# Channel statistics of a two-layer metaformer kernel, two pixels to an instruction

## The reference

```python
# layer 0
x = x + _L0_conv_ref(_ln_c(x), ...)      # patches of 3x3 pixels, best match of 512 vectors, a small MLP
t = _to_tokens(x); t = t + _L0_ffn_ref(_ln_t(t), W1, b1, W2, b2); x = _from_tokens(t, x)
# layer 1
x = x + _L1_conv_ref(_ln_c(x))           # x / (2 + 1e-4 * box5x5(sum over channels of x*x)) ** 0.75
t = _to_tokens(x); t = t + _L1_ffn_ref(_ln_t(t), W1, b1, W2, b2); x = _from_tokens(t, x)

def _ln_c(v, eps=1e-6):                  # over the 96 channels of one pixel; _ln_t the same with 1e-5
    m = jnp.mean(v, axis=1, keepdims=True); s = jnp.var(v, axis=1, keepdims=True)
    return (v - m) / jnp.sqrt(s + eps)
```

## Time and profile before

| | |
|---|---|
| median of 3 runs | 3355.06 us (3355.01 to 3362.01) |
| profiled execution | 3366.41 us, its span 3364.6 us |
| mean granted TensorE clock | 0.957 |
| busy: DVE, PE, ACT, POOL | 3022.2, 2824.8, 2608.5, 1192.6 us |
| DVE's statistics (L815) | 3456 instructions, 634.3 us |
| chain that ended last, by engine | DVE 36%, ACT 26%, PE 25%, DMA 7%, issue 5% |

### The profile page before, as it was taken

One profiled execution on the slowest core, in us unless ns is written; L12 is line 12 of the kernel. 1 busy time (PEld: TensorE's weight loads), 2 busy tenths in 40 slices (PEclk: granted clock), 3 DMA queues, 4 the chain that ended last, 5 costly groups with the idle time before them and its releaser, 6 DMA issues.

```text
span 3364.6 us, 55888 instructions
## 1 busy us (share of the span) xinstructions
PE 2824.8 (84%) x15886; PEld 1512.2 (45%) x15886; DVE 3022.2 (90%) x10843; ACT 2608.5 (78%) x7047; POOL 1192.6 (35%) x1159
## 2 busy tenths in 40 slices
PE   5888898988888888888888888888989899889654
PEld 2444444444445444444444444444444445444322
DVE  6888999999999999999999999999999999999532
ACT  0444788888888887878888788888888888888876
POOL 1223243333334333333433433334343434334221
PEclk9999999999999999999999999999999999999755
DMA  3111222222222222232232222223222223232111
GB/s 91 48 55 47 66 69 84 80 72 81 71 73 80 69 83 66 69 82 67 68 84 65 73 79 68 84 68 83 71 82 71 83 70 84 68 84 58 37 48 43
DMA packets 236607, 237.32 MB, mean 71 GB/s; under 512 B 183426, under 2 KB 186764, under 8 KB 236300
## 3 DMA queue, kind: packets, MB, share of 16 engines
q1 hardware_dynamic: 226060, 214.86, 23.2%
q0 software_dynamic: 10240, 18.89, 2.2%
HBM read 134.72 MB, written 57.02 MB: 57 GB/s over the span
## 4 chain that ended last, share of the span: by engine, by line
DVE 36%; ACT 26%; PE 25%; DMA 7%; issue 5%; SPq 0%; POOL 0%; POOLq 0%; DVEq 0%
ACT ffn_hid L552 11%; ACT ffn_x L585 10%; PE banks L415 10%; DVE st L815 7%; DMA ffn_xT<-ffn_x 7%; DVE ffn_hid L911 7%; DVE pix L824 6%; DVE ffn_hid L903 6%; PE banks L392 4%; PE banks L460 4%; PE banks L400 3%; DVE x L894 3%; PE banks L438 2%; ACT h L665 2%; ACT x L598 1%
## 5 line engine op out<-in xcount | busy, mean ns | idle before, releaser
L552 ACT ACTIVATE ffn_hid<-banks 128x512 f16<-128x512 f32 (+1 forms) x2304 | 1052.7, 492 | 387.3 <-PE banks L392 386.6
L415 PE MATMUL banks<-wcT,xc 128*128 128x512 f32 x2304 | 1217.8, 620 | 79.7 <-DVE pix L824 43.6
L392 PE MATMUL banks<-ffn_xT,w1q 128*128 128x512 fp8e5 (+1 forms) x2304 | 706.7, 340 | 260.1 <-ACT ffn_hid L552 170.4
L1080 POOL TENSOR_TENSOR x<-x,ffn_f 128x864 f32<-128x864 f32 x256 | 491.7, 1921 | 1038.5 <-DVE nb L777 920.3
L824 DVE TENSOR_REDUCE pix<-banks 128x1 f32<-128x512 f32 x1152 | 787.1, 684 | 69.0 <-PE banks L415 68.7
L392 PEld LDWEIGHTS banks<-ffn_xT,w1q 128*128 128x128 bf16 x2304 | 219.5, 98 | 783.7 <-ACT ffn_hid L552 541.5
L400 PE MATMUL banks<-w2q,ffn_hid 128*128 128x96 bf16 x6912 | 394.6, 211 | 160.7 <-DVE ffn_hid L911 159.9
L903 DVE TENSOR_SCALAR ffn_hid<-ffn_hid,b1q 128x1152 f16<-128x1152 f16 x768 | 419.3, 559 | 116.0 <-ACT ffn_hid L552 116.0
L400 PEld LDWEIGHTS banks<-w2q,ffn_hid 128*128 128x128 f16 x6912 | 353.1, 101 | 364.1 <-issue 335.0
L598 ACT ACTIVATE x<-x,cols 128x96 f32<-128x96 f32 x1152 | 511.7, 473 | 0.0
L585 ACT ACTIVATE ffn_x<-x,cols 128x96 fp8e5<-128x96 f32 x1152 | 501.4, 485 | 0.0
(11 more groups left out here) (137 smaller groups left out, 2849.9 us busy)
## 6 DMA issues: line engine op xcount, KB each, us to landing
xt<-x_tok_in SPq DMA_DIRECT2D x128, 432.0 KB
xc<-x_chan_in SPq DMA_DIRECT2D x128, 432.0 KB
out_tok<-x SPq DMA_DIRECT2D x128, 432.0 KB
ffn_xT<-ffn_x SPq DMA_TRANSPOSE x256, 2.6
win<-x_tok_in,xrow POOLq DMA_INDIRECT x128, 3.1
wrow<-vector_table,vidx POOLq DMA_INDIRECT x128, 2.7
shift<-shift_in SPq DMA_DIRECT2D x1, 960.0 KB
vector_table<-wtab SPq DMA_DIRECT2D x1, 384.0 KB, 2.9
```

The costliest lines, as they stand in the source:

```text
L392: last = pe.matmul(bank[:, 0:c1 - c0], w1q[:, ffn.layer, c * P:(c + 1) * P], pairs, start=True, stop=True)
L415: last = pe.matmul(ps_score[score_bank(j)], xc[p][:, j, :], wcT[:, :], start=True, stop=True)
L552: return nc.scalar.activation(dst, src, ACT.Copy)
L1080: tt(dst, x, ffn.f[:, :, :], ALU.add).then_inc(ready, 1)
```

## The change

The statistics take two pixels at a time. The source is read channel by channel and within a channel pixel by pixel, so that the even places are all of the first pixel and the odd places all of the second; the six values are then count, mean and sum of squared deviations of two pixels. They go straight into `pix`, by kind (plane 0 the counts, 1 the means, 2 the sums, 3 the roots), so `st3`, `mtmp`, `twice` and five operations of `moments` go. Nine pixels are five instructions; the fifth reads the last pixel twice and fills a tenth place that nobody uses. The groups of 3+6, 9 and 3+3+3 pixels become 2+3, 5 and 2+1+2 instructions. Means in place of doubled means change the factors to -1.0, and one operation of `mlp_input` (L876) goes. The wait on `kept` moves from `moments` to the front of the statistics of x2. The roots and their arguments are addressed as four rows of nine, where `pix` has rows of ten.

```diff
@@ -165,17 +165,16 @@
         xt = sb("xt", [P, XT, J, C])
         xc = [sb(f"xc_{i}", [P, J, P]) for i in range(2)]
 
-        st3 = sb("st3", [P, 3, J, 6])
-
-        pix = [sb(f"pix_{i}", [P, 3, 4, J]) for i in range(2)]
-        twice = [b[:, 0, 0:3, :] for b in pix]
-        ssq = [b[:, 1, 0:3, :] for b in pix]
-        roots = [b[:, 2, :, :] for b in pix]
-
-        mx = [b[:, 1, 1, :] for b in pix]
-        mtmp = sb("mtmp", [P, 2, 3, J])
+
+
+        pix = [sb(f"pix_{i}", [P, 4, 4, 2 * PAIRS]) for i in range(2)]
+        mean = [b[:, 1, 0:3, 0:J] for b in pix]
+        ssq = [b[:, 2, 0:3, 0:J] for b in pix]
+        roots = [b[:, 3, :, 0:J] for b in pix]
+
+        mx = [b[:, 2, 1, 0:J] for b in pix]
         args = sb("args", [P, 4, J])
-        rtmp = sb("rtmp", [P, 4 * J])
+        rtmp = sb("rtmp", [P, 4, J])
         nb1 = sb("nb1", [P, J])
         sim = [sb(f"sim_{i}", [P, J]) for i in range(2)]
         top = [sb(f"top_{i}", [P, 8]) for i in range(2)]
@@ -206,7 +205,7 @@
 
 
         img = sb("img", [P, 3, SLOTS, J])
-        twice_i, ssq_i, rstd_i = (img[:, i, :, :].rearrange("p s j -> p (s j)") for i in range(3))
+        mean_i, ssq_i, rstd_i = (img[:, i, :, :].rearrange("p s j -> p (s j)") for i in range(3))
         r2_i, sq_i = sb("r2_i", [P, SLOTS * J]), sb("sq_i", [P, SLOTS * J])
 
         cols_i = sb("cols_i", [P, 4, SLOTS, J])
@@ -696,7 +695,8 @@
             nc.vector.memset(pow_half[:], -0.5)
             nc.vector.memset(eps[:, 0, :], 1e-5)
             nc.vector.memset(eps[:, 1:3, :], 1e-6)
-            nc.vector.memset(st3[:], 0.0)
+            for b in pix:
+                nc.vector.memset(b[:], 0.0)
             for c in chosen:
                 nc.vector.memset(c[:], 0.0)
 
@@ -770,49 +770,36 @@
                 if k.back is not None:
                     wait_past(dve, ffn0.x8_ready, k.back)
                 rc.begin(k.moments)
-                flat = lambda b: b.rearrange("p a j -> p (a j)")
-                y = flat(roots[k.p])
-                yield from inverse_root(rc, flat(args[:, :, :]), y, rtmp[:, :])
+                yield from inverse_root(rc, args[:, :, :], roots[k.p], rtmp[:, :, :])
                 rc.wait()
-                nc.vector.scalar_tensor_tensor(out=nb1[:, :], in0=twice[k.p][:, 0, :], scalar=-0.5,
+                nc.vector.scalar_tensor_tensor(out=nb1[:, :], in0=mean[k.p][:, 0, :], scalar=-1.0,
                                                in1=roots[k.p][:, 0, :], op0=ALU.mult,
                                                op1=ALU.mult).then_inc(root_ready, 1)
                 yield
 
-            MOMENTS = 7
+            MOMENTS = 2
             mc = Chain(dve, mom_chain, MOMENTS)
 
             def moments(tile, p):
-
 
                 dve.wait_ge(stats_ready, tile + 1)
                 wait_past(dve, root_ready, tile)
-                wait_past(dve, kept, tile - 6)
                 mc.begin(tile)
-                of = lambda i: st3[:, :, :, i]
-                d, m2 = mtmp[:, 0, :, :], mtmp[:, 1, :, :]
-                mc.add(nc.vector.tensor_tensor(d, of(1), of(4), ALU.subtract),
-                       nc.vector.tensor_tensor(m2, of(2), of(5), ALU.add))
-                yield
-                mc.wait()
-                mc.add(nc.vector.tensor_tensor(d, d, d, ALU.mult))
-                yield
-                mc.add(nc.vector.tensor_tensor(twice[p], of(1), of(4), ALU.add))
-                yield
-                mc.wait()
-                mc.add(nc.vector.scalar_tensor_tensor(out=ssq[p], in0=d, scalar=C / 4.0, in1=m2, op0=ALU.mult,
-                                                      op1=ALU.add))
-                yield
-                mc.wait()
                 mc.add(nc.vector.scalar_tensor_tensor(out=args[:, 0:3, :], in0=ssq[p], scalar=1.0 / C,
                                                       in1=eps[:, :, :], op0=ALU.mult, op1=ALU.add),
                        nc.vector.tensor_copy(args[:, 3, :], ssq[p][:, 1, :]))
                 assert mc.done == mc.per
                 yield
 
-            def group_stats(which, src, j0, j1, between):
-                for j in range(j0, j1):
-                    last = nc.vector.bn_stats(st3[:, which, j, :], src[:, j, :])
+            def group_stats(which, src, k, i0, i1, between):
+
+                if which == 2 and i0 == 0:
+                    wait_past(dve, kept, k.stats - 6)
+                for i in range(i0, i1):
+                    two = src[:, 2 * i:2 * i + 2, :] if 2 * i + 1 < J else src[:, J - 1:J, :].broadcast_to([P, 2, C])
+                    last = nc.vector.bn_stats(
+                        pix[k.q][:, 0:3, which, 2 * i:2 * i + 2].rearrange("p f t -> p t f"),
+                        two.rearrange("p t c -> p c t"))
                     run(between, 1)
                 return last
 
@@ -848,13 +835,13 @@
                 yield
                 f1c.wait()
                 one = pick[p][:, :].rearrange("p (o j) -> p o j", o=1).broadcast_to([P, 3, J])
-                f1c.add(nc.vector.tensor_tensor(junk[:, :, :], pix[p][:, :, 1, :], one, ALU.mult))
+                f1c.add(nc.vector.tensor_tensor(junk[:, :, :], pix[p][:, 1:4, 1, 0:J], one, ALU.mult))
                 yield
                 f1c.wait()
                 nc.vector.tensor_reduce(chosen[p][:, 0:3], junk[:, :, :], AX.X, ALU.add).then_inc(pick_ready, 1)
                 yield
 
-            f3c = Chain(dve, f3_chain, 6)
+            f3c = Chain(dve, f3_chain, 5)
 
             def win_vector(f2, q, between):
 
@@ -873,13 +860,12 @@
                 f3c.begin(f3)
                 f3c.add(nc.vector.tensor_reduce(dots[:, :], prod_dot[:, :, :], AX.X, ALU.add),
                         nc.vector.tensor_scalar(mix[:, 0:1], chosen[q][:, 2:3], top_q, None, ALU.mult),
-                        nc.vector.tensor_scalar(mix[:, 2:3], chosen[q][:, 0:1], 0.5, None, ALU.mult),
                         nc.vector.tensor_scalar(mix[:, 1:2], top_q, -1.0, 1.0, ALU.mult, ALU.add))
                 meanwhile()
                 f3c.wait()
 
                 f3c.add(nc.vector.tensor_tensor(inp[:, C:C + J], dots[:, :], roots[q][:, 3, :], ALU.mult),
-                        nc.vector.tensor_scalar(wnorm[:, :], win[q][:, :], mix[:, 2:3], mix[:, 0:1],
+                        nc.vector.tensor_scalar(wnorm[:, :], win[q][:, :], chosen[q][:, 0:1], mix[:, 0:1],
                                                 ALU.subtract, ALU.mult))
                 f3c.wait()
                 run(between, 1)
@@ -945,7 +931,7 @@
                 yield
                 lc.wait()
                 lc.add(nc.vector.tensor_scalar(alpha, rg, 1.0, None, ALU.add),
-                       nc.vector.scalar_tensor_tensor(out=beta, in0=twice_i, scalar=-0.5, in1=rg,
+                       nc.vector.scalar_tensor_tensor(out=beta, in0=mean_i, scalar=-1.0, in1=rg,
                                                       op0=ALU.mult, op1=ALU.mult))
                 yield
                 lc.wait()
@@ -961,7 +947,7 @@
                 yield from inverse_root(lc, arg, rstd, t)
                 lc.wait()
                 assert lc.done == lc.per
-                nc.vector.scalar_tensor_tensor(out=bias, in0=twice_i, scalar=-0.5, in1=rstd, op0=ALU.mult,
+                nc.vector.scalar_tensor_tensor(out=bias, in0=mean_i, scalar=-1.0, in1=rstd, op0=ALU.mult,
                                                op1=ALU.mult).then_inc(lrn_ready, 1)
                 yield
 
@@ -996,10 +982,10 @@
                 scores(2, WIN_TURN, factors, 2)
                 if k.fs is not None:
                     dve.wait_ge(xt_loaded[k.p], landed(k.fs, k.p))
-                    last = group_stats(1, xt[:, k.fs & XT - 1], 0, 3, factors)
+                    last = group_stats(1, xt[:, k.fs & XT - 1], k, 0, 2, factors)
                 if k.tail is not None:
                     dve.wait_ge(x2_ready, k.tail + 1)
-                    last = group_stats(2, x2[:, k.tail & RING - 1], 0, J, factors)
+                    last = group_stats(2, x2[:, k.tail & RING - 1], k, 0, PAIRS, factors)
                 if k.f2 is not None:
                     win_vector(k.f2, k.q, factors)
                 relu(ffn1, k.rear, 0)
@@ -1009,21 +995,21 @@
                 scores(5, 6, factors, 2)
                 round_up(ffn1, k.rear)
                 if k.fs is not None:
-                    last = group_stats(1, xt[:, k.fs & XT - 1], 3, J, factors)
+                    last = group_stats(1, xt[:, k.fs & XT - 1], k, 2, PAIRS, factors)
                 run(factors)
                 if k.f3 is not None:
                     residual1(k.f3, k.q)
                 scores(6, 7)
                 if k.f3 is not None:
                     dve.wait_ge(x1_ready, k.f3 + 1)
-                    group_stats(0, x1[k.q], 0, 3, iter(()))
+                    group_stats(0, x1[k.q], k, 0, 2, iter(()))
                 scores(7, 8)
                 if k.f3 is not None:
-                    group_stats(0, x1[k.q], 3, 6, iter(()))
```

(5 more changed lines are left out.)

## The result

| | before | after |
|---|---|---|
| median of 10 runs | 3359.06 us (3355.01 to 3365.66) | 3369.64 us (3362.88 to 3379.74) |
| ratio to before | | 1.0031, 95% interval 1.0018 to 1.0043 |
| profiled execution, its span | 3366.41, 3364.6 us | 3371.26, 3369.5 us |

What follows compares the result with a forecast made beforehand. DVE was busiest (3022 of 3364.6 us), with regular steps also closing through PE and ACT within some 0.1 us. Terms +62, -2, -8, -11 and -4 gave +37 on 3355: 3392 us, range 3305 to 3440 at about 0.8.

Steps and rivals of the forecast that it cites:

- The price of the statistics: BN_STATS on DVE: 192 values read alternately run at full rate, 344 ns, saving 0.44 us a step.
- The rival by hop cost: Alternating read on DVE pays for every hop, 460 ns per statistics instruction: 3351 us, chance 0.25.
- The race: DVE's rounding L911 against POOL's product L1075: index and product come 0.19 us earlier, so 35 more steps are lost.
- The tipping point: Lead at which POOL's product goes ahead of DVE's rounding: between zero and 0.1 us for POOL.
- 35 x (24.85 - 23.08) = +62 us: Regular steps: 35 of 44 races won by little flip, each step growing from 23.08 to 24.85 us.
- -0.3 each: The 27 regular steps already lost get shorter through fewer statistics, together -8 us.
- the joins: Five DVE operations removed between relu units of ffn0: 0.55 us of work, hidden behind ACT but for 0.1 us.
- the -8 and -2 of the sum: Regular steps: -8 us for 27 already lost, -2 for 9 still won and some 14 with a late vector.
- 14 x -0.3 = -4: Ramp and tail steps: 0.3 us less each, together -4 us.
- Image steps: 28 steps, two of eight, where the product comes too late to race: -0.4 us each, so -11 us.
- The race is still won: DVE's rounding still goes first in the 44 steps: 3325 us at full rate, or 3300; chance 0.18.
- 27 x -2.1 = -57: If the index comes 0.1 us later, the 27 lost steps are won too: -57 us, giving 3300.

Runs made afterwards that it cites:

- after_split32: Changed kernel with the five statistics of xt split 3+2 in place of 2+3, one moving ahead of the vector index: 3334.0 us, 0.9912.
- before_early: Kernel before, with the ninth statistics instruction of x2 moved from ahead of the vector index to behind it: 3359.7 us, 0.9996.
- before_nojoins: Kernel before without the five joining operations, so the norms are not computed: 3339.0 us, 0.9936.
- before_early2: Kernel before, with the ninth statistics instruction of x2 moved behind the first two relu operations of ffn1: 3414.7 us, 1.0163.
- before_order: Kernel before, with a wait that holds POOL's product until the rounding of ffn1 of the same step is done: 3318.8 us, 0.9883.
- after_joins: Changed kernel with five operations of 27 values, results unused, put where the joins stood: 3382.9 us, 1.0048.
- after_order: Changed kernel, with a wait that holds POOL's product until the rounding of ffn1 of the same step is done: 3283.9 us, 0.976.
- after_half: Changed kernel with POOL's product taken over four of the nine pixels: 3296.7 us, 0.9808.

## Why the prediction was right in its mechanism and too large in its size

**The price of the statistics** was right. I had the choice between 344 ns (full rate) and 460 (a hop on every value, after L794), and took the lower: 353. The rival by hop cost is out. The rule of the 16-byte lines that I cited from the Trainium skill, "SBUF — State Buffer", Specifications, does not show in this read: it never hits a line twice in a row, yet costs 0.02 ns a value (353 against 349 ns for 192). The page "Vector Engine (DVE) Microarchitecture Reference" of the Trainium skill, section 5.2, fits with its one-source operation that alternates between two regions at the full rate; here the regions are 384 bytes apart. L794's 17 ns over L798 were no price of its stride that BN_STATS shares.

**The race** was right: index 0.18 us earlier (0.19 forecast), rounding at the same place, 40 more races lost (35 forecast), 68 in all for a forecast of 62. The tipping point, between a lead of 0 and one of 0.1 us for POOL, can be narrowed over all traces: the product starting 0.026 us ahead of the rounding still had to stand back (after_split32), 0.029 us ahead it went first (before_early, before_nojoins). One link was wrong without consequence: I wrote that the product follows the index by a gather. It follows the relu pair behind the index (before_early and before_early2). In the change both move together.

**The term that was mis-sized** is "35 x (24.85 - 23.08) = +62 us". I took the length of a lost step from lost steps of the kernel before, and all 28 of those were steps that were late already when they lost: the rounding starts 12.94 us or more into them, not 12.65. In the step of the earlier trace rows the rounding starts 0.57 us later than in that of the earlier trace rows, the index ends only 0.30 later, because part of the delay goes into the wait for POOL's x2. So POOL comes to lead: lateness and loss go together in the kernel before, and both were in my one number.

The changed kernel has 44 lost steps that came on time, 24.28 us each (12.65 to the rounding, 2.81 in it, 8.82 behind it), and 24 late ones, 24.81 each. In the work of the kernel before, before_early2 gives 24.72 for the first kind. So turning a race costs 24.72 - 23.09 = 1.6 us and not 2.15, and a lost step that came on time gains 0.44 from the change. For a late one I had "-0.3 each", and 25.15 to 24.81 is near it, though by another cause: I counted the statistics, and before_nojoins shows the joins. The sum put the joins at next to nothing, since "They sit between relu units of ffn0, where ACT holds the last L903 back". That is what a won step shows, where before_nojoins gains 0.1. A lost step comes out of the rounding 1.76 us late, and there the joins alone were 0.44. A cover was read in one kind of step and used for the other.

With 24.28, 35 steps give +42 in place of +62, and with the -8 and -2 of the sum regular steps come to +32; measured +29. In full: 40 x (24.28 - 23.16, the mean of a step not lost before) = +44.5; four lost steps that no longer come late, -3.5; the 24 late ones, -8.2; the 18 still not lost -3.7, 0.2 each and not the 0.1 of the sum. Together +29.1.

**The ramp** is the second term, "14 x -0.3 = -4": it gave 17.5 us. I had not looked at a ramp step. PE in one, from the kernel before and then from the changed one:

```profile
200.93 0.80 PE L400 MATMUL banks<-w2q,ffn_hid 128*128 128x96 bf16 x15 [1.89 <-DVE ffn_hid L911]
201.56 1.58 PE L415 MATMUL banks<-wcT,xc 128*128 128x512 f32 x2
202.93 1.17 PE L400 MATMUL banks<-w2q,ffn_hid 128*128 128x96 bf16 x12
```

```profile
149.95 0.80 PE L399 MATMUL banks<-w2q,ffn_hid 128*128 128x96 bf16 x15 [1.25 <-DVE ffn_hid L897]
150.58 1.09 PE L414 MATMUL banks<-wcT,xc 128*128 128x512 f32 x2
151.51 0.67 PE L399 MATMUL banks<-w2q,ffn_hid 128*128 128x96 bf16 x12
```

Before, the pause ahead of the output units is 1.89 us long and the matmuls behind it are slower, 1.58 us for the two of a score in place of 1.09. The granted clock of the ramp (third figure from the end):

```profile
60.00:370.00 310.00, 257.07 (x1080) 128.47 (x1081) 258.04 (x1009) 127.36 (x337) 82.37 (x80) 0.92 0.20 53
```

```profile
60.00:352.00 292.00, 248.05 (x1079) 124.77 (x1080) 245.35 (x776) 127.09 (x336) 82.45 (x80) 0.95 0.21 55
```

It is 0.92 before and 0.95 after: 11 stretches at the lower of TensorE's two levels (1.2 in place of 2.4 GHz) before, 6 after. Among the ramp's second to tenth steps those with one are 1.2 to 2.3 us longer than the shortest. A step without one has 21.92 us before (also in before_order) and 21.11 after. So of 17.5 us some 10 are in the steps themselves and the rest comes from fewer slow stretches. What sets their number is open: with operations put back where the joins were (after_joins) the pause is 1.44 us and 7 stretches are slow. In before_order, whose ramp is instruction for instruction that of the kernel before, there were 8 in place of 11, and the ramp had 298.9 us in place of 304.9. So part of the 17.5 belongs to that one execution: between the two kernels with the order fixed the ramp gained 11.6. With 298.9 for the ramp before, the two profiled spans would differ by 10.9 us in place of 4.9, an estimate that is near the 10.6 between the medians. The term was mis-sized by 8 to 14 us either way. **Image steps** gave 4.8 us for 11 expected; this I did not pursue.

**The rivals.** "The race is still won" was 3325 us at full rate, with the 27 lost races of before still lost; no run has just that case. after_order wins these too, by construction, and shows 3284. The prediction's price for winning them was 27 x -2.1 = -57; before_order won all 28 and brought 41. It remains true that the change is good and its consequence bad: 35 us gained at fixed order, 45 lost by turned races.

## What to carry to other kernels

Where two engines can exclude each other, who comes first is part of the schedule: look for the same instruction with two lengths (median 1059, maximum 2830), find what runs in the difference, and fix the order with a wait before tuning anything ahead of it. Otherwise a saving of 0.2 us can cost 1.6 us a step, and one that is worth 0.4 in one kind of step can look like nothing in another. And when a step's price is read from a population, see first whether its members share another trait than the one to be priced.

## What the runs showed of the hardware

- DVE's rounding (16-bit, in place, all in SBUF) and POOL's tensor_tensor exclude each other in whole instructions: 1.06 us becomes 2.8 behind a product of 2.01 us and 1.75 behind one of 1.00 us (after_half); the product becomes 2.9 behind the rounding. The second to come waits; by these traces POOL needs a lead of between 0.026 and 0.029 us to go first.
- A gather issued on POOL is held by DVE's relu pair (16-bit, in SBUF): 0.98 us becomes 1.14 when it starts 0.16 us earlier and the pair does not, and it ends 0.40 to 0.41 us behind the pair in either case.
- BN_STATS of 192 values read alternately from two pixels has 353 ns, in a row 349, of 96 values 243.
